# Cross-attention matmul and low-rank feed-forward layer: variance sums of a column in parts, and conversions, additions and low parts divided anew among the engines

## Chip, cores and metric

One core of one Trainium2 chip. The metric is the device time of the kernel in microseconds (us), the median of three runs.

## The reference

Two layers with a layernorm ahead of each (B = 2, 1024 positions, width 2048; everything is float32). The first multiplies the quantized layernorm with a quantized context, the second is a dense product with a bias and a low-rank part of 8 experts of rank 16, of which the two with the highest router probability count for each position:

```python
def fake_quant(x, s, z):                      # 0..255
    return (clip(round(x / s + z), 0, 255) - z) * s

x = x + matmul(fake_quant(_layernorm(x), s1, z1), fake_quant(ctx_4096, s2, z2))

y = _layernorm(x)
probs = softmax(y @ W_router.T)               # 8 experts
w = the two highest probs, divided by their sum
h = einsum('td,erd->ter', y, lora_A)          # r = 16
x = x + y @ W_base.T + b_base + einsum('ter,eor,te->to', h, lora_B, w) * 2.0
```

## The kernel before, in words

**Order of work.** Five programs are written out by hand, one for each engine (`sync_program`, `tensor_program`, `scalar_program`, `vector_program`, `pool_program`): each is a list of calls of small functions, and each function begins with its waits. Tables at the head of the file say which engine does a call that several could do ('a' ScalarE, 'd' VectorE, 'p' GpSimd): `QUANT` and `BACK` (first layer's activations), `CTXQ` and `CONV` (quantization and conversion of the context), `SQ0` and `SUM0` (additions for the second layernorm's statistics), `YLO` and `WLO` (low parts). An engine runs its list strictly in order, so a wait holds up all that stands behind it. SyncE (SP) issues nearly all loads and stores; GpSimd issues the stores of the output and some accumulating transfers on a queue of its own.

**Layer 1.** Batch 0 has 8 tiles of 128 positions, batch 1 too. For each: load (`xn_load`, 512 KB twice), statistics on VectorE (`ln1_stats` L572, L577), coefficients on GpSimd (`ln1_coef` L582 to L592), quantization to uint8 (`ln1_quant`, L606 on ScalarE, L608 on VectorE), 16 transposes of a block of 128 on TensorE (`ln1_turn` L624, four instructions since the uint8 are turned as f32), write-back of the turned tile as bf16 (`ln1_back`, L634 ScalarE, L636 VectorE). The context comes in 32 tiles of 1 MB (`ctx_load`; 16 for a batch), each quantized (`ctx_quant`, L652 ScalarE, L654 VectorE) and converted to bf16 (`ctx_conv`, L661 ScalarE, L663 VectorE and GpSimd). There are two load buffers, two uint8 buffers and two bf16 buffers (and a third for tile 2). `gemm1` (L683) takes 32 products of 512 columns for a tile (two banks of 512 positions, 16 blocks of the width); the first three tiles are done in quarters of 256 positions, as the turned tiles become ready. `evac1` (L698 VectorE, L695 ScalarE) adds the residual to a bank.

**Second layernorm, batch 0.** Beside the later products of layer 1, the 16 tiles of x are summed (`add0`, L713 VectorE, L709 GpSimd) and so are the squares of the values less a shift (`shift0`, `square0` L771, `sqadd0` L779). `mean` (L746) multiplies the sum with a constant matrix; `centre0` (L785) subtracts it from the tiles. `var_total(0)` (L822) multiplies the two sums, block by block, with one column of that matrix: 16 products of one column (32 instructions, f32 takes two each). `var_offset`, `var_add`, `var_root`, `var_diag` and `var_spread` make the scale of each position from them. The norms of the low-rank and router matrices (`a_root`, `r_root`) lie nearby. For batch 1, `var_total(1)` has one sum: 8 products, 16 instructions.

**Layer 2.** Each batch has 8 pairs of 128 + 128 outputs (numbers 0 to 7 and 8 to 15), and each pair is done as a block product of seven instead of eight: the operands of the activations (B11, T1, B21, B22, T2, T3, T4, each 2 MB with both parts) and of the weights are sums and differences (`y_diff` L989 to L1006, `w_add` L1383 to L1396), each split in an fp16 high part (`y_high`, `w_high` L1403, ScalarE) and low part (`y_low` L1013, `w_low` L1409, on VectorE or GpSimd). `product` is 8 blocks by three products of 512 columns (L1451 to L1453), 24 for each of the seven. Weights come by `raw_load` (1 MB), `w_squares` and `w_norm` (L1319) make a norm that `w_total` (L864, TensorE) sums, `w_scale` (L1358) scales. The low-rank product `lora_h` (L1068 to L1070) of the second batch reads 2 MB loads of the operands (`y_load`) that `yd_store` has put away earlier; `tail` adds the low-rank part to a pair, `post` (L1507, L1513, L1515) combines and evacuates, and `store` (L536, GpSimd) sends 512 KB to the output.

## Time and profile before

| | |
|---|---|
| median of three runs | 965.16 us |
| lowest, highest | 964.08, 966.11 us |
| the profiled execution's own time | 965.27 us |
| its span (first to last instruction) | 963.5 us |
| TensorE busy | 926.9 us (96% of the span) |
| VectorE, ScalarE, GpSimd busy | 583.1 (61%), 506.8 (53%), 309.5 us (32%) |
| mean granted TensorE clock | 0.998 of full speed |
| read from HBM, written | 137.44 MB, 56.62 MB |

The profile is of one execution on one core. Times within it are counted from the span's start. Its parts name an instruction by engine, line of the kernel, operation and the tiles that it writes and reads; PE is TensorE, PEld its weight loads, DVE VectorE, ACT ScalarE, POOL GpSimd, SP SyncE. "[2.45 <-DVE S L663]" behind an instruction says that the engine was idle for 2.45 us before it and what ended that: VectorE's line 663 writing tile S. A DMA's time to landing runs from its issue to its last packet.

### The profile page before, as it was taken

The numbers are of one execution on the slowest core, as the hardware profiler recorded it, in microseconds if no ns is written. First come the engines' busy times: TensorE is split into PE (matmuls) and PEld (weight loads), VectorE is DVE, ScalarE is ACT, GpSimd is POOL, SyncE is SP. The second block draws the span as 40 slices with busy tenths as digits, with TensorE's granted clock in tenths as the row PEclk, the third lists the DMA queues.
The fourth block names the chain that finished last, engine by engine and source line by source line (L and its number), as shares of the span: only waits on it lengthen the run. The fifth ranks groups of instructions, "written<-read, shape, count | busy, mean of one in ns | idle before, by whom it ended". The sixth has DMA issues, their size and how long they took to land.

```text
span 963.5 us, 12922 instructions
## 1 busy us (share of the span) xinstructions
PE 926.9 (96%) x4518; PEld 438.4 (45%) x4538; DVE 583.1 (61%) x730; ACT 506.8 (53%) x494; POOL 309.5 (32%) x249
## 2 busy tenths in 40 slices
...
GB/s 309 361 357 363 336 328 326 299 276 292 282 127 106 231 231 229 245 112 260 176 232 265 177 230 186 332 318 237 103 34 116 50 93 65 99 126 71 88 66 44
DMA packets 61444, 197.07 MB, mean 205 GB/s; under 512 B 5696, under 2 KB 22208, under 8 KB 52928
## 3 DMA queue, kind: packets, MB, share of 16 engines
...
HBM read 137.44 MB, written 56.62 MB: 201 GB/s over the span
## 4 chain that ended last, share of the span: by engine, by line
PE 58%; issue 6%; DVE 3%; DMA 2%; POOL 2%; ACT 1%; DVEq 0%; POOLq 0%; ACTq 0%; SPq 0%
PE PS L1451 17%; PE PS L1452 17%; PE PS L1453 17%; PE PS L1464 1%; PE PS L1466 1%; PE PS L1465 1%; DMA out_dram<-Q 1%; PE PS L1144 1%; DMA S<-in_wT_dram 1%; PE PS L1068 1%; PE PS L1069 1%; PE PS L1070 1%; POOL S L1409 1%; DVE S L790 0%; DVE XA L1013 0%
## 5 line engine op out<-in xcount | busy, mean ns | idle before, releaser
L1451 PE MATMUL PS<-XA,Q 128*128 128x512 f16 x384 | 145.6, 379 | 0.0
L1453 PE MATMUL PS<-XA,Q 128*128 128x512 f16 x384 | 145.6, 379 | 0.0
L1452 PE MATMUL PS<-XA,Q 128*128 128x512 f16 x384 | 145.6, 379 | 0.0
L1409 POOL TENSOR_TENSOR S<-S 128x1024 f16<-128x1024 f32 x29 | 64.5, 2228 | 166.8 <-ACT S L1403 166.8
L683 PE MATMUL PS<-Q,S 128*128 128x512 bf16 x502 | 112.5, 382 | 2.9 <-DVE S L698 2.2
L683 PE MATMUL PS<-EX,S 128*128 128x512 bf16 (+1 forms) x534 | 107.1, 359 | 4.0 <-DVE S L663 2.5
L1403 ACT ACTIVATE Q<-S 128x1024 f16<-128x1024 f32 x64 | 66.6, 1050 | 71.4 <-PE PS L1453 29.2
L1358 ACT ACTIVATE S<-S,WC 128x1024 f32<-128x1024 f32 x64 | 70.8, 1138 | 51.2 <-DMA S<-in_wT_dram 35.3
L1451 PE MATMUL PS<-EX,S 128*128 128x512 f16 x256 | 97.0, 379 | 0.1
L1453 PE MATMUL PS<-EX,S 128*128 128x512 f16 x256 | 97.0, 379 | 0.0
L1452 PE MATMUL PS<-EX,S 128*128 128x512 f16 x256 | 97.0, 379 | 0.0
L1409 DVE TENSOR_TENSOR Q<-S,Q 128x1024 f16<-128x1024 f32 x52 | 65.1, 1262 | 41.4 <-ACT Q L1403 41.2
L1403 ACT ACTIVATE S<-S 128x1024 f16<-128x1024 f32 x48 | 49.6, 1050 | 74.7 <-DVE S L1387 26.3
L1507 DVE SCALAR_TENSOR_TENSOR Q<-PS,WC,Q 128x512 f32<-128x512 f32 x36 | 26.9, 749 | 94.4 <-PE PS L1466 77.7
L683 PEld LDWEIGHTS PS<-Q,S 128*128 128x128 bf16 x512 | 50.4, 99 | 64.7 <-issue 4.8
L683 PEld LDWEIGHTS PS<-EX,S 128*128 128x128 bf16 x544 | 53.9, 99 | 54.2 <-DVE S L663 2.8
L652 ACT ACTIVATE S<-S,cst 128x2048 uint8<-128x2048 f32 x31 | 64.4, 2086 | 19.0 <-DMA S<-in_cT_dram 18.7
L536 POOL DMA_DIRECT2D out_dram<-Q x30 | 26.5, 941 | 121.6 <-DVE Q L1515 64.8
L1409 POOL TENSOR_TENSOR Q<-S,Q 128x1024 f16<-128x1024 f32 x12 | 29.5, 2463 | 90.2 <-ACT Q L1403 90.2
L1451 PEld LDWEIGHTS PS<-XA,Q 128*128 128x128 f16 x384 | 37.6, 98 | 45.7 <-issue 1.1
L1453 PEld LDWEIGHTS PS<-XA,Q 128*128 128x128 f16 x384 | 37.6, 98 | 45.3
L1452 PEld LDWEIGHTS PS<-XA,Q 128*128 128x128 f16 x384 | 37.6, 98 | 44.9 <-issue 0.3
...
## 6 DMA issues: line engine op xcount, KB each, us to landing
...
out_dram<-Q POOLq DMA_DIRECT2D x30, 512.0 KB, 5.6
EX<-in_xn_dram SPq DMA_DIRECT2D x24, 512.0 KB, 6.4
...
XA<-in_xT_dram SPq DMA_DIRECT2D x16, 512.0 KB, 8.3
out_dram<-XA SPq DMA_DIRECT2D x16, 512.0 KB, 7.4
out_dram<-S SPq DMA_DIRECT2D x16, 512.0 KB, 4.3
```

The lines of the kernel that those rows point to most:

```text
L536: e.dma_start(outT[b, o], ob[(2 * i + h) % 3], accum_op=ALU.add).then_inc(stored.of(2 * i + h), 16)
L652: e.activation(u8b[g % 2], ctx_f[g % 2], ACT.Identity, bias=z2, scale=inv2).then_inc(ctxq.of(g), 1)
L683: last = e.matmul(bank(a)[:, t0 % 512:t0 % 512 + t1 - t0], q2[q][:, 128 * k:128 * (k + 1)], q1T[b][:, k, t0:t1], start=(k == 0), stop=(k = ...
L1068: e.matmul(bank(banks[n]), hi[:, c], yh(op, k), start=(k == 0 and op != B22), stop=False)
L1069: e.matmul(bank(banks[n]), hi[:, c], yl(op, k), start=False, stop=False)
L1358: e.activation(v, v, ACT.Copy, bias=0.0, scale=w_cols(i)[:, 4:5]).then_inc(w_scaled.of(i, q), 1)
L1403: e.activation(ring[slot_of(i, n)][:, 0:1024], W_SRC[n], ACT.Copy, bias=0.0, scale=1.0).then_inc(w_hi.of(i, n), 1)
L1409: e.tensor_tensor(v[:, 1024:2048], W_SRC[n], v[:, 0:1024], ALU.subtract).then_inc(w_lo.of(i, n), 1)
L1451: e.matmul(bank(bk), wh, yh(op, k), start=(fresh and k == 0), stop=False, skip_group_check=not fresh)
L1452: e.matmul(bank(bk), wh, yl(op, k), start=False, stop=False, skip_group_check=not fresh)
L1453: last = e.matmul(bank(bk), wl, yh(op, k), start=False, stop=(read and k == 7), skip_group_check=not fresh)
L1507: e.scalar_tensor_tensor(dst, src, kk, dst, op0=ALU.mult, op1=ALU.add).then_inc(post_ok.of(i, n), 1)
```

## The change

- `var_total` is split: for batch 0 the sums of the offset become `offset_total(p)`, those of the squares `var_total(0, p)`, for batch 1 `var_total(1, p)`, with p = 0 and 1, each for four blocks. In `tensor_program` the four calls of batch 0 stand in a row, 16 products earlier than before, and the two of batch 1 in a row. What waited for the one signal waits for the ones that it needs.
- SyncE issues the loads of context tiles 0 and 1 directly behind activation tiles 0 to 3, ahead of tile 4; later loads, stores and reloads stand in another order in places.
- ScalarE, VectorE and GpSimd share quantizations, write-backs, conversions, additions, squares' additions and low parts in another way. Calls before and after: VectorE's conversions 7 and 1, context quantizations 1 and 7, write-backs 9 and 5, quantizations 2 and 6, `add0` 0 and 3, `sqadd0` 0 and 4, `w_low` 71 and 97, `y_low` 55 and 42. ScalarE's conversions 18 and 17, context quantizations 31 and 25, write-backs 9 and 13, quantizations 14 and 10. GpSimd's conversions 7 and 14, `add0` 14 and 11, `sqadd0` 15 and 11, `w_low` 41 and 15, `y_low` 9 and 22.
- `warm` is defined and called nowhere. The tables of layer 2 and the programs' other lines are in another order in places; the diff is cut to its core.

```diff
--- before.py
+++ after.py
-QUANT = {'a': [(0, 1), (0, 2), (0, 3), (0, 4), (0, 5), (0, 6), (1, 0), (1, 1), (1, 2), (1, 3), (1, 4), (1, 5), (1, 6), (1, 7)],
-    'd': [(0, 0), (0, 7)]}
-BACK = {'a': [(0, 0, 0), (0, 1, 0), (0, 3, 1), (0, 2, 0), (0, 4, 0), (0, 6, 0), (0, 7, 1), (1, 0, 0), (1, 4, 0)],
-    'd': [(0, 3, 0), (0, 5, 0), (0, 7, 0), (1, 2, 0), (1, 1, 0), (1, 3, 0), (1, 5, 0), (1, 6, 0), (1, 7, 0)]}
-CTXQ = {'a': [0, 2, 3, 4, 5, 6, 7, 8, 9, 10, 11, 12, 13, 14, 15, 16, 17, 19, 18, 20, 21, 22, 23, 24, 25, 26, 28, 27, 29, 30,
-    31], 'd': [1]}
-CONV = {'a': [7, 9, 12, 13, 14, 15, 16, 17, 18, 21, 22, 25, 26, 27, 28, 29, 30, 31], 'd': [0, 2, 3, 6, 10, 11, 23], 'p': [1, 4,
-    5, 8, 19, 20, 24]}
+QUANT = {'a': [(0, 1), (0, 3), (0, 4), (0, 5), (0, 7), (1, 2), (1, 4), (1, 5), (1, 6), (1, 7)], 'd': [(0, 0), (0, 2), (0, 6),
+    (1, 0), (1, 1), (1, 3)]}
+BACK = {'a': [(0, 0, 0), (0, 2, 0), (0, 3, 1), (0, 3, 0), (0, 4, 0), (0, 5, 0), (0, 6, 0), (0, 7, 1), (1, 1, 0), (1, 4, 0),
+    (1, 6, 0), (1, 5, 0), (1, 7, 0)], 'd': [(0, 1, 0), (0, 7, 0), (1, 0, 0), (1, 2, 0), (1, 3, 0)]}
+CTXQ = {'a': [0, 3, 4, 5, 7, 9, 8, 10, 12, 13, 15, 14, 16, 18, 20, 19, 22, 24, 25, 26, 27, 28, 29, 30, 31], 'd': [1, 2, 6, 11,
+    17, 21, 23]}
+CONV = {'a': [3, 7, 8, 9, 11, 14, 15, 17, 19, 20, 22, 23, 25, 26, 28, 29, 30], 'd': [31], 'p': [0, 1, 2, 4, 5, 6, 10, 12, 13,
+    16, 18, 21, 24, 27]}
...
-SQ0 = {'d': [], 'p': [1, 2, 3, 4, 5, 6, 7, 8, 9, 10, 11, 12, 13, 14, 15]}
-SUM0 = {'d': [], 'p': [1, 2, 3, 4, 5, 6, 7, 9, 10, 11, 12, 13, 14, 15]}
+SQ0 = {'d': [1, 3, 7, 11], 'p': [2, 4, 5, 6, 8, 9, 10, 12, 13, 14, 15]}
+SUM0 = {'d': [7, 9, 14], 'p': [1, 2, 3, 4, 5, 6, 10, 11, 12, 13, 15]}
...
     centred1 = signal("centred1", range(NT))
     cd_out = loaded("cd_out", range(NT), 2)
     sq1_ok = signal("sq1", range(1, NT))
-    var_sum = signal("var_sum", range(NB))
+    off_sum = signal("off_sum", range(2))
+    var_sum = signal("var_sum", [(b, p) for b in range(NB) for p in range(2)])
     var_off = signal("var_off", range(2))
     var_eps = signal("var_eps", range(NB))
@@ -640,6 +641,15 @@
             e.wait_ge(*back[b, i, part])
 
 
+    def warm(e, n, at=None):
+        e.wait_ge(*const["mean"])
+        if at is not None:
+            e.wait_ge(*xn_in[0, at, 1])
+        v = mean_w[:, :].bitcast(BF16)[:, 0:128]
+        for _ in range(n):
+            e.matmul(bank(3)[:, 0:128], v, v, start=True, stop=True)
+
+
     def q2_place(g):
         return 2 if g == 2 else g % 2
 
@@ -656,7 +666,8 @@
     def ctx_conv(e, g):
         e.wait_ge(*ctxq[g])
         if g >= 3:
-            e.wait_ge(*gemm[{3: 1, 4: 0}.get(g, g - 2), 1])
+            for h in range(2):
+                e.wait_ge(*gemm[{3: 1, 4: 0}.get(g, g - 2), h])
         if g in CONV["a"]:
             e.activation(q2[q2_place(g)], u8b[g % 2], ACT.Copy, bias=-128.0, scale=1.0).then_inc(conv.of(g), 1)
         else:
@@ -807,7 +818,15 @@
         e.wait_ge(*sq1_ok[i])
         e.tensor_tensor(acc1, acc1, sq1[i % 2], ALU.add).then_inc(acc1_ok.of("sq", i), 1)
 
-    def var_total(e, b):
+    def offset_total(e, p):
+
+        e.wait_ge(*sum0[NT - 1])
+        e.wait_ge(*back[1, 6, 0])
+        for t in range(4 * p, 4 * p + 4):
+            last = e.matmul(bank(4)[:, TT + t:TT + t + 1], acc0[:, 128 * t:128 * (t + 1)], mean_w[:, 0:1], start=True, stop=True)
+        last.then_inc(off_sum.of(p), 1)
+
+    def var_total(e, b, p):
 
         at, acc = (bank(6), acc1) if b else (bank(4), accD)
         if b:
@@ -815,22 +834,21 @@
             e.wait_ge(*centred1[15])
         else:
             e.wait_ge(*sqsum0[15])
-            e.wait_ge(*sum0[NT - 1])
             e.wait_ge(*back[1, 6, 0])
-        for src, c in ((acc, 0),) if b else ((acc, 0), (acc0, TT)):
-            for t in range(TT):
-                last = e.matmul(at[:, c + t:c + t + 1], src[:, 128 * t:128 * (t + 1)], mean_w[:, 0:1], start=True, stop=True)
-        last.then_inc(var_sum.of(b), 1)
+        for t in range(4 * p, 4 * p + 4):
+            last = e.matmul(at[:, t:t + 1], acc[:, 128 * t:128 * (t + 1)], mean_w[:, 0:1], start=True, stop=True)
+        last.then_inc(var_sum.of(b, p), 1)
 
     def var_offset(e):
-        e.wait_ge(*var_sum[0])
+        e.wait_ge(*off_sum[1])
+        e.wait_ge(*var_sum[0, 1])
         e.tensor_scalar(rr[:, TT:2 * TT], bank(4)[:, TT:2 * TT], 1.0, None, op0=ALU.mult).then_inc(var_off.of(0), 1)
         e.wait_ge(*var_off[0])
         e.tensor_tensor(rr[:, TT:2 * TT], rr[:, TT:2 * TT], rr[:, TT:2 * TT], ALU.mult).then_inc(var_off.of(1), 1)
 
     def var_add(e, b):
         if b:
-            e.wait_ge(*var_sum[1])
+            e.wait_ge(*var_sum[1, 1])
             e.tensor_scalar(rr[:, 0:TT], bank(6)[:, 0:TT], EPS, None, op0=ALU.add).then_inc(var_eps.of(1), 1)
         else:
             e.wait_ge(*var_off[1])
@@ -985,7 +1003,7 @@
                 e.wait_ge(*y_lo[0, k - 1, "T"])
                 e.wait_ge(*y_hi[0, k - 1, "T"])
             else:
-                e.wait_ge(*var_sum[0])
+                e.wait_ge(*var_sum[0, 1])
         e.tensor_tensor(TX[:, 512:1024], B[:, 512:1024], A[:, 512:1024], ALU.subtract).then_inc(y_diff.of(b, k, 3), 1)
 
     def y_diff1(e, b, k):
@@ -1045,7 +1063,8 @@
             e.wait_ge(*prod[7, 1])
         else:
             e.wait_ge(*turned[1, 7])
-            e.wait_ge(*var_sum[0])
+            e.wait_ge(*off_sum[1])
+            e.wait_ge(*var_sum[0, 1])
         e.scalar_tensor_tensor(lo[:, v], src[:, v], s_a, hi[:, v], op0=ALU.mult, op1=ALU.subtract).then_inc(a_lo.of(b, c), 1)
 
     def lora_h(e, b, ks):
@@ -1091,7 +1110,7 @@
                                    op0=ALU.mult, op1=ALU.add).then_inc(h_ok.of(b, s), 1)
 
     def r_clear(e):
-        e.wait_ge(*var_sum[0])
+        e.wait_ge(*off_sum[1])
         for s in range(2):
             e.memset(r_ab[0][s], 0.0).then_inc(r_zero.of(s), 1)
 
@@ -1302,7 +1321,7 @@
                 e.wait_ge(*conv[30])
                 e.wait_ge(*conv[31])
                 e.wait_ge(*turned[1, 7])
-                e.wait_ge(*var_sum[0])
+                e.wait_ge(*off_sum[1])
             e.activation(junk, raw[h], ACT.Square, accum_out=col_[:, h:h + 1]).then_inc(w_sq.of(j, h), 1)
         e.wait_ge(*b_in[j])
         if j >= 2:
...
     def sync_program(e, general):
-        xn_load(e, 0, 4); ctx_load(e, 0); ctx_load(e, 1); xn_load(e, 0, 5); ctx_load(e, 2); xn_load(e, 0, 6)
-        xn_load(e, 0, 7); x_load(e, 1, general); ctx_load(e, 3); x_load(e, 0, general); x_load(e, 2, general)
...
+        ctx_load(e, 0); ctx_load(e, 1); xn_load(e, 0, 4); x_load(e, 0, general); xn_load(e, 0, 5); ctx_load(e, 2)
+        xn_load(e, 0, 6); xn_load(e, 0, 7); ctx_load(e, 3); xn_load(e, 1, 0); x_load(e, 2, general); xn_load(e, 1, 1)
+        ctx_load(e, 4); x_load(e, 1, general); x_load(e, 3, general); x_load(e, 4, general); ctx_load(e, 5)
+        xn_load(e, 1, 2); ctx_load(e, 6); xn_load(e, 1, 3); ctx_load(e, 7); x_load(e, 8, general); x_load(e, 7, general)
...
-        yd_store(e, 7, 6); yd_store(e, 7, 1); yd_store(e, 7, 7); yd_store(e, 7, 5); a_reload(e); b_load(e, 8); y_load(e, 0)
+        yd_store(e, 7, 1); a_reload(e); yd_store(e, 7, 2); b_load(e, 8); yd_store(e, 7, 6); yd_store(e, 7, 3)
+        yd_store(e, 7, 5); yd_store(e, 7, 4); yd_store(e, 7, 7); raw_load(e, 8, 1); y_load(e, 0); raw_load(e, 8, 0)
...
     def tensor_program(e):
         ln1_turn(e, 0, 0); ln1_turn(e, 0, 1); ln1_turn(e, 0, 2); ln1_turn(e, 0, 3); gemm1(e, 0, 0, 256, 0, 16)
...
-        gemm1(e, 18, 0, 512, 0, 8); gemm1(e, 18, 512, 1024, 0, 8); var_total(e, 0); gemm1(e, 18, 0, 512, 8, 16)
...
-        tail(e, 2, 1); tail(e, 2, 3); var_total(e, 1); product(e, 3, 0); var_spread(e, 1); product(e, 3, 1)
...
+        gemm1(e, 17, 512, 1024, 8, 16); r_total(e); gemm1(e, 17, 0, 512, 8, 16); offset_total(e, 0); offset_total(e, 1)
+        var_total(e, 0, 0); var_total(e, 0, 1); gemm1(e, 18, 512, 1024, 0, 8); gemm1(e, 18, 512, 1024, 8, 16)
...
+        product(e, 2, 6); tail(e, 2, 1); var_total(e, 1, 0); var_total(e, 1, 1); product(e, 3, 0); var_spread(e, 1)
...
     def scalar_program(e):
-        ln1_quant(e, 0, 1); ln1_back(e, 0, 0, 0); ln1_quant(e, 0, 2); ln1_back(e, 0, 1, 0); ln1_quant(e, 0, 3)
-        ctx_quant(e, 0); ln1_back(e, 0, 3, 1); ln1_back(e, 0, 2, 0); ln1_quant(e, 0, 4); ctx_quant(e, 2); ln1_quant(e, 0, 5)
...
+        ln1_quant(e, 0, 1); ln1_back(e, 0, 0, 0); ctx_quant(e, 0); ln1_quant(e, 0, 3); ln1_back(e, 0, 2, 0)
+        ln1_back(e, 0, 3, 1); ln1_back(e, 0, 3, 0); ln1_quant(e, 0, 4); ln1_quant(e, 0, 5); ln1_back(e, 0, 4, 0)
...
     def vector_program(e):
         ln1_stats(e, 0, 0); ln1_stats(e, 0, 1); ln1_quant(e, 0, 0); ln1_stats(e, 0, 2); ln1_stats(e, 0, 3)
-        ln1_stats(e, 0, 4); ln1_back(e, 0, 3, 0); ctx_conv(e, 0); ctx_quant(e, 1); ln1_stats(e, 0, 5); ln1_stats(e, 0, 6)
-        ctx_conv(e, 2); ln1_stats(e, 0, 7); ln1_back(e, 0, 5, 0); ln1_quant(e, 0, 7); ln1_back(e, 0, 7, 0); evac1(e, 1, 0)
...
+        ln1_quant(e, 0, 2); ln1_back(e, 0, 1, 0); ctx_quant(e, 1); ln1_stats(e, 0, 4); ln1_stats(e, 0, 5); ctx_quant(e, 2)
+        ln1_stats(e, 0, 6); ln1_stats(e, 0, 7); evac1(e, 0, 0); ln1_quant(e, 0, 6); ln1_stats(e, 1, 0); evac1(e, 2, 0)
...
     def pool_program(e, general):
-        ln1_coef(e, 0, 0); ln1_coef(e, 0, 1); ln1_coef(e, 0, 2); ln1_coef(e, 0, 3); ln1_coef(e, 0, 4); ctx_conv(e, 1)
-        ln1_coef(e, 0, 5); ln1_coef(e, 0, 6); ln1_coef(e, 0, 7); ln1_coef(e, 1, 0); ctx_conv(e, 4); ln1_coef(e, 1, 1)
...
+        ln1_coef(e, 0, 0); ln1_coef(e, 0, 1); ln1_coef(e, 0, 2); ln1_coef(e, 0, 3); ctx_conv(e, 0); ctx_conv(e, 1)
+        ln1_coef(e, 0, 4); ln1_coef(e, 0, 5); ctx_conv(e, 2); ln1_coef(e, 0, 6); ln1_coef(e, 0, 7); ln1_coef(e, 1, 0)
...
+        ctx_conv(e, 12); sqadd0(e, 8); ctx_conv(e, 13); add0(e, 10); ln1_coef(e, 1, 7); sqadd0(e, 9); sqadd0(e, 10)
+        add0(e, 11); add0(e, 12); ctx_conv(e, 16); sqadd0(e, 12); add0(e, 13); sqadd0(e, 13); add0(e, 15); ctx_conv(e, 18)
+        sqadd0(e, 14); a_root(e); sqadd0(e, 15); r_clear(e); r_root(e); var_root(e, 0); add1(e, 2); ctx_conv(e, 21)
...
+        w_low(e, 7, 3); store(e, 6, 0); y_low(e, 1, 7, "A"); store(e, 7, 0); store(e, 7, 1); w_low(e, 8, 4); store(e, 8, 1)
...
```

## Rows read from the trace of the kernel before

**Rows 1.** Page, part 1: busy us of each engine (share of the span), instructions:
```profile
PE 926.9 (96%) x4518; PEld 438.4 (45%) x4538; DVE 583.1 (61%) x730; ACT 506.8 (53%) x494; POOL 309.5 (32%) x249
```

**Rows 2.** Waits of TensorE: line waiting <- releaser: us in all, how many, longest:
```profile
PE PS L683 <- DVE S L698: 2.2, 2, 1.2
PE PS L864 <- DVE WC L1319: 2.1, 1, 2.1
```

**Rows 3.** Windows: us; busy PE, PEld, DVE, ACT, POOL; PE clock, DMA share, GB/s:
```profile
0.00:28.91 28.91, 4.47 (x17) 2.87 (x17) 17.98 (x37) 14.49 (x9) 9.08 (x34) 1.00 0.82 297
28.91:60.00 31.09, 30.04 (x234) 24.09 (x236) 25.46 (x37) 20.02 (x11) 12.16 (x27) 1.00 0.97 377
60.00:169.40 109.40, 108.85 (x505) 51.33 (x513) 80.03 (x100) 84.02 (x56) 84.97 (x65) 1.00 0.90 341
622.00:963.50 341.50, 338.19 (x1634) 154.04 (x1632) 127.72 (x146) 109.08 (x119) 60.77 (x38) 1.00 0.40 112
```

**Rows 4.** TensorE's timeline: start, us, instructions in a row [idle before <- releaser]:
```profile
25.34 1.12 PE L624 MATMUL PS<-ident,S 128*128 128x128 f32 x4 [2.63 <-ACT S L606]
...
28.91 9.09 PE L683 MATMUL PS<-EX,S 128*128 128x256 bf16 x64 [2.45 <-DVE S L663]
...
43.80 1.91 PE L683 MATMUL PS<-EX,S 128*128 128x256 bf16 x16 [0.99 <-ACT EX L634]
...
58.16 0.60 PE L624 MATMUL PS<-ident,S 128*128 128x128 f32 x4
...
215.40 20.88 PE L683 MATMUL PS<-Q,S 128*128 128x512 bf16 x94 [0.92 <-DVE S L698]
```

**Rows 5.** Timelines of ScalarE and of VectorE, first 28 us:
```profile
15.70 2.09 ACT L606 ACTIVATE XA<-EX,mv 128x2048 uint8<-128x2048 f32 x1 [9.85 <-POOL mv L592]
17.70 1.85 ACT L634 ACTIVATE EX<-PS 128x2048 bf16<-128x2048 uint8 x1
...
27.17 2.77 ACT L634 ACTIVATE EX<-PS 128x1024 bf16<-128x1024 uint8 x2
...
12.85 1.28 DVE L608 TENSOR_SCALAR S<-EX,mv 128x2048 uint8<-128x2048 f32 x1
...
16.72 2.40 DVE L572 BATCH_NORM_STATS2 st<-XA 128x6 f32<-128x512 f32 x4
```

**Rows 6.** DMA issues, 3 to 6 us: KB each, us to landing:
```profile
XA<-in_xn_dram SPq DMA_DIRECT2D x4, 512.0 KB, 10.1
```

**Rows 7.** Timelines and windows around the variance sums, and GpSimd's last additions:
```profile
157.00 1.96 PE L746 MATMUL PS<-S,mean_w 128*128 128x512 f32 x4
...
169.46 3.73 PE L822 MATMUL PS<-mean_w,S 128*128 128x1 f32 x32
...
169.40:176.30 6.90, 6.66 (x41) 4.80 (x41) 6.83 (x9) 3.52 (x2) 0.00 (x0) 0.75 0.97 354
...
426.00:428.00 2.00, 2.00 (x11) 0.88 (x9) 0.50 (x1) 0.00 (x0) 2.00 (x1) 1.00 0.00 0
...
157.28 4.86 POOL L779 TENSOR_TENSOR S<-S 128x1024 f32<-128x1024 f32 x2 [0.99 <-ACT S L771]
```

**Rows 8.** ScalarE's timeline, the eviction ahead of the norm's squares:
```profile
366.32 0.78 ACT L1513 ACTIVATE Q<-PS,bo,WC 128x512 f32<-128x512 f32 x1 [3.13 <-DMA out_dram<-Q]
```

**Rows 9.** GpSimd's timeline, three stores; DMA issues, 640 to 672 us:
```profile
647.85 2.66 POOL L536 DMA_DIRECT2D out_dram<-Q  x3
...
EX<-yops_dram SPq DMA_DIRECT2D x1, 2048.0 KB, 18.8
```

**Rows 10.** Groups by line and form: busy, mean ns | idle before; and VectorE's timeline:
```profile
L709 POOL TENSOR_TENSOR S<-S,XA 128x1024 f32<-128x1024 f32 x6 | 15.0, 2498 | 7.3 <-DVE XA L698 7.1
...
L663 POOL TENSOR_SCALAR S<-S 128x2048 bf16<-128x2048 uint8 x7 | 13.3, 1898 | 11.0 <-DVE S L654 6.3 <-PE PS L683 4.2 <-ACT S L652 0.4
...
L1387 DVE TENSOR_TENSOR S<-S 128x1024 f32<-128x1024 f32 x1 | 1.2, 1225 | 0.0
...
626.46 3.14 DVE L1387 TENSOR_TENSOR S<-S 128x1024 f32<-128x1024 f32 x1 [12.07 <-POOL Q L1409]
```

642 lines of the change are left out of this document (318 added, 324 removed), and 88 rows, old and new, of tables (EVAC, GEMM, POST, PROD).

## Prediction

> **What bounds the kernel now.** I read the busy line of the page first. TensorE is busy for 926.9 of 963.5 us [rows 1], so another engine changes the time only by making TensorE wait or by ending later than it. What can change is the idle 36.6 us, and the clock that TensorE runs at. Next come its waits: the longest outside the start are 2.2 us in two waits for evictions by VectorE and 2.1 us in one wait for a norm [rows 2]. The windows say where the rest lies [rows 3]: 4.47 us of work in the first 28.91 us, 1.05 us idle up to 60 us, 0.55 us idle in the 109.4 us after that. So 25.5 of the 36.6 us lie before 60 us, and there I expect the change to count. About 3.3 us are the last eviction and store, whose chain stays. The timeline of TensorE gives the shape of the start [rows 4]: the last of four groups of transposes at 25.34, a wait of 2.45 us for VectorE's conversion, 64 quarter-width products from 28.91, an idle 0.99 us before 43.80, then no gap to 58.16.
>
> **The change, part by part.** TensorE gets no new work: two calls of the variance sums become six of half or a quarter of the length, with the same 48 instructions. All else is another order and another sharing out. Durations are from the profiled execution, 965.27 us by its own clock, 0.11 above the median of the three runs; I sum against it and take the 0.11 off.
>
> *The start.* Before, ScalarE alternates quantizations of 2.09 us and write-backs of 1.85 us for the first tiles [rows 5], and the context tile is converted after them. Now VectorE quantizes tile 2 and writes back tile 1, and GpSimd converts context tiles 0 and 1. I replay it with the old durations. VectorE begins the statistics of tile 3 at 16.72 and is through at 19.4 (2.40 and a short aggregation); it quantizes tile 2 in 1.28 us (20.7); it then has 4.1 us to write back tile 1, for which ScalarE took 1.85. ScalarE ends its first quantization at 17.8 and the write-back of tile 0 at 19.6 as before, then takes context tile 0 (21.6) and tile 3 (23.7). GpSimd converts the context tile by 23.5 (1.90 us [rows 10]). The transposes of tile 3, 1.12 us, end at 24.8, and the first products start there instead of at 28.91. The second quarter needs tiles 2 and 3 written back, 1.85 and 2.77 us on ScalarE from 23.7, so 28.3. The 64 products took 9.09 us; with a wait of 0 to 1.2 us in them they end at 33.9 to 35.1, before at 38.0. Behind them two groups of transposes and 32 products (9.09 / 2 = 4.5 us at this rate) cover two write-backs (3.7), so the idle 0.99 goes too. At equal work that is 3.6 to 4.8 us early. I take 3.6, the low end, since the low clock of the first products may stretch over the wait.
>
> This rests on the loads. Before, the first two context loads were issued behind tile 4's, which waits for the first quantization; now they follow tile 3's directly. Loads of tiles 2 and 3 took 10.1 us to land [rows 6], because they stood behind those of tiles 0 and 1: the queue was full. Tile 3's landed by 16.72, when its statistics begin without a wait [rows 5], so it was issued at about 6, and the new ones will be too. If the new ones stay behind them, at 377 GB/s [rows 3] one megabyte takes 2.8 us: tile 3 at about 16, context tile 0 at 19, before ScalarE asks for it at 19.6, tile 4 at 24, when VectorE is free for its statistics. The queue has more to do early and later loads gain as TensorE does.
>
> *From 60 to 169 us* TensorE had 0.55 us idle. Here VectorE gives up six conversions and four write-backs and takes four quantizations, six of the context and seven additions; GpSimd takes seven conversions and gives up the seven additions. A context buffer is free when the tile two before is done, and its conversion is due one tile of products later: 94 products took 20.88 us [rows 4], so 32 take 7.0 us. A conversion of 1.90 and two additions of 2.5 [rows 10] just fit. I cost it at nothing; what it costs uncovered is the second rival.
>
> *The variance sums of batch 0.* 32 instructions of one column took 3.73 us, and the granted clock over the 6.9 us from their start was 0.75 [rows 7], so 1.7 us went at the level of 1.2 GHz instead of 2.4. The new functions split the sums in four parts, but the new order puts the four calls next to each other, with no product between; the same in batch 1, where 16 instructions stood together and the clock stayed at 1.00 behind them [rows 7]. So the lost time stays: 0, between -1.9 (no fall, no idle 0.2 us behind it) and 0. The sums also come 16 products earlier. Their squares were complete at 162.14, 7.3 us ahead. Now GpSimd's last addition stands behind a root that waits for VectorE after the mean: 1.96 us of mean, 1.22 of centring, some 0.7 of column work, 2.43 of addition [rows 7, 10], 6.3 us in all, while TensorE has 24 products (5.3) and the offset half of the sums (1.9), 7.2. It fits by 0.9; uncovered by one more addition it costs 1.6.
>
> *The other waits.* Evictions: VectorE gives up three low parts of the activations in that stage and gets three of the weights: 0, between -2.2 and +2.2. The norm wait of 2.1 us came from an eviction on ScalarE that waited for an output buffer until 366.32 [rows 8], ahead of the squares. The new order keeps that, puts both evictions of the pair in front (+0.7) and calls for the norm three products earlier (+0.7), but GpSimd reaches the store slightly sooner: 0, between -2.1 and +1.4.
>
> *The second low-rank product* is fed by 2 MB loads just ahead of TensorE. Three stores that GpSimd issued at 647.85, behind these loads, made the one beside them take 18.8 us [rows 9], against 8.4 for its own and the megabyte before it at 377 GB/s: 3.5 us for each store. Two of them now go out during the loads that TensorE is waiting for. On the other side the reload ahead of these loads is issued earlier. I take +0.5, between 0 and +3.5.
>
> *Low parts.* 26 of the weights' 41 on GpSimd go to VectorE and 13 of the activations' the other way. VectorE is busy for 127.72 of the last 341.5 us [rows 3]; nothing.
>
> **Sum:** -3.6 + 0.5 = -3.1; 965.27 - 3.1 - 0.11 = 962.1 us.
>
> **Where rule and trace part.** GpSimd's additions took 2.5 us on average, and one of VectorE 3.14 where the same line took 1.22 elsewhere, while GpSimd worked beside it [rows 10]: a collision costs up to 1.9 us, and few show. The Trainium skill, "SBUF — State Buffer", section "Who interferes with whom", says that a VectorE instruction with two SBUF inputs and a GpSimd instruction that reads SBUF shut each other out for a whole instruction, which speaks against sharing work out between these two. By that rule any overlap in the first 170 us counts, and the term set at nothing above would be some us, as in the second rival.
>
> **Rivals.** (1) *The gain is given back at a later wait*, the low-rank product's or an eviction's. For: loads with no slack. Against: the earlier reload. 962.1 + 2.3 = 964.4. (2) *Conversions on GpSimd become TensorE's wait; slower.* Place: context tiles 4 to 21. Behind two additions (5.0), the factors of a tile (1.7) and one collision (1.9), a conversion of 1.9 ends 10.5 us after its release, 3.5 late. Two such cases give 962.1 + 7.0 = 969.1. Point: a single one leaves 965.6, no change. Against: the new order rarely puts two additions there. (3) *The early context loads share the queue with tiles 2 and 3* instead of standing behind them: 2 MB, up to 5.6 us later for tile 3, and the start gains nothing or loses 1: 962.1 + 4 = 966.1. Against: loads queued behind others did land in turn. (4) *The clock does not fall after the sums* though they stand together, as in batch 1: 962.1 - 1.9 = 960.2. That the announced split does not take place is part of the forecast.
>
> **Chances.** Forecast 0.44 (its own range 959.9 to 963.6), rival 1 0.20, 2 0.14, 3 0.08, 4 0.14. A measurement of this kernel tells 0.2%, 1.9 us, from no change. Faster: nearly all of the forecast and the fourth, 0.56; slower: the second and half of the third, 0.18; same: the rest, 0.26. The range leaves out the far end of the second rival and gains beyond both bounds: 957.8 to 968.0.
>
> **What would show it.** Right: first product at 24.5 to 26 us, no idle before 44, all 32 sums in a row at about 163 us and 1.2 GHz behind them. Wrong: product waits released by GpSimd's conversions; waits of the second low-rank product for loads; statistics of tile 2 or 3 that wait for their load.

## The result, and the profile after it

The changed kernel takes 973.04 us (median of 13 runs, 967.86 to 977.63), the kernel before 966.11 us (13 runs): a ratio of 1.0068, with a 95% interval of 1.0045 to 1.0090. It is slower by 0.7%, where I forecast faster by 0.3%.

The busy line of the changed kernel's page, against [rows 1]:

```profile
PE 930.1 (96%) x4538; PEld 438.5 (45%) x4538; DVE 622.7 (64%) x750; ACT 491.7 (51%) x487; POOL 277.3 (29%) x236
```

Its waits of TensorE (line that waits, what released it: us in all, times, longest), against [rows 2]:

```profile
PE PS L1087 <- DMA XA<-yops_dram: 5.3, 2, 4.9
PE PS L694 <- DVE S L709: 4.6, 1, 4.6
...
PE PS L882 <- DVE WC L1338: 1.5, 1, 1.5
PE PS L1087 <- ACT S L706: 1.4, 1, 1.4
PE PS L1087 <- DVE S L709: 1.2, 1, 1.2
```

The profiled execution's span is 971.4 us, 7.9 more than before. Idle time outside TensorE's work is 971.4 - 930.1 = 41.3 us, 4.7 more than before, although the start is shorter. The other 3.2 us are in the busy time itself: the same work at a lower clock. The windows show both (columns as in [rows 3]: stretch, its us, busy PE, PEld, DVE, ACT, POOL, clock, DMA share, GB/s):

```profile
0.00:25.09 25.09, 4.26 (x17) 3.00 (x18) 18.70 (x33) 10.18 (x6) 10.61 (x30) 1.00 0.92 349
...
60.00:162.00 102.00, 101.67 (x478) 47.65 (x476) 78.92 (x92) 73.91 (x51) 74.59 (x59) 1.00 0.90 342
...
225.00:276.00 51.00, 43.73 (x191) 18.88 (x189) 43.40 (x48) 33.15 (x33) 24.46 (x13) 0.93 0.79 258
...
622.00:971.40 349.40, 340.70 (x1636) 154.33 (x1634) 148.94 (x166) 110.25 (x120) 16.12 (x17) 1.00 0.38 109
...
230.00:240.00 10.00, 5.39 (x16) 2.00 (x16) 9.11 (x11) 4.63 (x7) 3.71 (x3) 0.66 1.03 360
638.59:642.60 4.01, 4.01 (x11) 1.50 (x12) 0.80 (x1) 0.00 (x0) 0.00 (x0) 0.57 1.05 399
```

The first 170 us are as good as forecast. The time goes in two places, near 230 us and near 638 us, and each has a stretch of low clock behind it. TensorE's timeline says where it stands at each point:

```profile
24.18 1.11 PE L625 MATMUL PS<-ident,S 128*128 128x128 f32 x4 [2.55 <-ACT S L607]
25.09 8.48 PE L694 MATMUL PS<-EX,S 128*128 128x256 bf16 x64
...
35.27 0.66 PE L625 MATMUL PS<-ident,XA 128*128 128x128 f32 x4 [1.26 <-ACT XA L607]
...
162.17 1.84 PE L826 MATMUL PS<-mean_w,S 128*128 128x1 f32 x16
163.88 1.93 PE L839 MATMUL PS<-mean_w,S 128*128 128x1 f32 x16
165.66 20.88 PE L694 MATMUL PS<-Q,S 128*128 128x512 bf16 x96
186.62 1.95 PE L739 MATMUL PS<-S,mean_w 128*128 128x512 f32 x4
188.41 41.60 PE L694 MATMUL PS<-Q,S 128*128 128x512 bf16 x192
234.62 37.05 PE L694 MATMUL PS<-Q,S 128*128 128x512 bf16 x160 [4.61 <-DVE S L709]
272.89 0.38 PE L1087 MATMUL PS<-XA,S 128*128 128x512 f16 x1 [1.22 <-DVE S L709]
...
275.14 0.39 PE L1087 MATMUL PS<-XA,S 128*128 128x512 f16 x1 [1.44 <-ACT S L706]
...
638.59 0.42 PE L1087 MATMUL PS<-XA,Q 128*128 128x512 f16 x1 [4.92 <-DMA XA<-yops_dram]
```

First products: 25.09 for 28.91 us, 3.8 ahead. In this execution no half clock follows the sums. At 230.0 us the wait begins. The 160 products behind it took 37.05 us; 96 of them took 20.88 from 165.66, which is 34.8 for 160. (The 94 in 20.88 us of [rows 4] are 96 too, with two records missing.) The clock events of the trace (its two levels are 1.2 and 2.4 GHz) show 1.2 GHz for 6.8 us from 233 us and for 3.4 us from 639 us, and nowhere else between 28 us, where the first event raises the clock, and the end. Half of 10.2 us is 5.1 us, of which some fell into the waits themselves.

At 230 us VectorE had this behind it (its timeline):

```profile
222.63 2.95 DVE L1031 TENSOR_TENSOR XA<-S,XA 128x1024 f16<-128x1024 f32 x1
225.50 4.36 DVE L1128 SCALAR_TENSOR_TENSOR S<-Braw,cst,S 128x128 f16<-128x128 f32 x1
229.78 1.21 DVE L983 TENSOR_TENSOR S<-XA,PS 128x1024 f32<-128x1024 f32 x1
...
233.07 1.40 DVE L709 SCALAR_TENSOR_TENSOR S<-PS,cst,S 128x512 f32<-128x512 f32 x2
```

GpSimd's timeline beside it:

```profile
211.34 1.09 POOL L518 DMA_DIRECT2D S<-in_xT_dram  x1 [0.37 <-issue]
...
222.14 2.35 POOL L733 TENSOR_TENSOR S<-S 128x1024 f32<-128x1024 f32 x1 [7.52 <-DMA S<-in_xT_dram]
...
225.41 2.43 POOL L1031 TENSOR_TENSOR EX<-S,EX 128x1024 f16<-128x1024 f32 x1
227.54 2.16 POOL L674 TENSOR_SCALAR S<-S 128x2048 bf16<-128x2048 uint8 x1
```

`r_low` (L1128), a tile of 128 by 128, starts when GpSimd starts a low part and ends when the conversion behind it ends: 4.36 us. Ahead of it another VectorE operation stretched to 2.95 us over GpSimd's addition. The two evictions of context tile 25, for which TensorE waits, stand behind.

### The profile page after: what moved, and what is told of

It reads as the page before. It is cut to its first block, busy times and chain, and to the rows that moved or that the text cites. A ratio compares the mean times of both kernels' runs of the same rounds, so it can differ in the third digit from the quotient of the medians.

```text
span 971.4 us, 12949 instructions
## 1 busy us (share of the span) xinstructions
PE 930.1 (96%) x4538; PEld 438.5 (45%) x4538; DVE 622.7 (64%) x750; ACT 491.7 (51%) x487; POOL 277.3 (29%) x236
## 4 chain that ended last, share of the span: by engine, by line
PE 42%; DMA 3%; issue 3%; DVE 1%; POOL 1%; ACT 0%; SPq 0%; DVEq 0%; POOLq 0%
PE PS L1470 12%; PE PS L1471 12%; PE PS L1472 12%; DMA XA<-yops_dram 2%; PE PS L1483 1%; PE PS L1485 1%; PE PS L1484 1%; DMA S<-in_wT_dram 1%; PE PS L1163 0%; POOL S L1031 0%; PE PS L1088 0%; PE PS L1087 0%; PE PS L1089 0%; DVE Q L1068 0%; DVE S L1007 0%
## 5 line engine op out<-in xcount | busy, mean ns | idle before, releaser
L1428 DVE TENSOR_TENSOR Q<-S,Q 128x1024 f16<-128x1024 f32 x55 | 71.3, 1304 | 63.0 <-ACT Q L1422 63.0
L1428 DVE TENSOR_TENSOR S<-S 128x1024 f16<-128x1024 f32 x42 | 50.4, 1220 | 17.1 <-ACT S L1422 17.0
L662 ACT ACTIVATE S<-S,cst 128x2048 uint8<-128x2048 f32 x25 | 52.1, 2086 | 15.0 <-DMA S<-in_cT_dram 12.8
L1534 DVE TENSOR_SCALAR Q<-PS,WC,bo 128x512 f32<-128x512 f32 x27 | 21.8, 807 | 42.7 <-PE PS L1485 21.5
```

The costliest lines, as they stand in the source:

```text
L662: e.activation(u8b[g % 2], ctx_f[g % 2], ACT.Identity, bias=z2, scale=inv2).then_inc(ctxq.of(g), 1)
L1428: e.tensor_tensor(v[:, 1024:2048], W_SRC[n], v[:, 0:1024], ALU.subtract).then_inc(w_lo.of(i, n), 1)
L1534: e.tensor_scalar(dst, src, kk, bcol, op0=ALU.mult, op1=ALU.add).then_inc(post_ok.of(i, n), 1)
```

## The experiments

Sixteen kernels, in the order in which they ran; lines of an edit are cut to the calls that move. "Clock" is the mean over a kernel's runs of the granted clock. Where it is set against a time, the loss is (1 - clock) times the span: for the changed kernel's 13 runs 6.4 us at a mean clock of 0.9935; for the kernel before, in the 26 runs shared by the first four experiments, 2.7 us at 0.9972. So of the 7 us between them up to 3.7 are clock: where a fall lies over a wait it costs nothing.

Each ratio is against runs of the kernel before taken beside that kernel; their medians were 966.7 (e1 to e4), 965.1 (e5 to e8), 966.4 (e9 to e11), 965.3 (e12 to e14) and 964.7 us (e15, e16), so medians of different groups can be up to 2 us apart for no reason of the kernels, and the ratios are the safer comparison. The profiled execution is one run of its kernel and not always a typical one: those of e4_start (959.0 us), e5 (973.2) and e10 (963.7) are the fastest of their kernels, that of e11 (973.8) the slowest, and that of e16 (972.4) is 6.8 us above its median. One of e7's 12 runs took 3760.9 us; it is left out of its clock, and leaving it out of the median changes 0.01 us.

| kernel | median us | ratio to before (95%) | clock |
|---|---|---|---|
| changed | 973.0 | 1.0068 (1.0045 to 1.0090) | 0.9935 |
| e1_evac | 975.5 | 1.0076 (1.0049 to 1.0103) | 0.9920 |
| e2_stores | 970.6 | 1.0041 (1.0015 to 1.0067) | 0.9937 |
| e3_both | 971.5 | 1.0051 (1.0025 to 1.0076) | 0.9945 |
| e4_start | 962.7 | 0.9957 (0.9932 to 0.9981) | 0.9978 |
| e5_rlow | 978.6 | 1.0141 (1.0115 to 1.0168) | 0.9912 |
| e6_rlow_st | 972.3 | 1.0074 (1.0045 to 1.0103) | 0.9935 |
| e7_split | 971.2 | 1.0061 (1.0041 to 1.0082) | 0.9960 |
| e8_oldearly | 967.4 | 1.0012 (0.9991 to 1.0034) | 0.9970 |
| e9_sp | 976.6 | 1.0100 (1.0073 to 1.0128) | 0.9907 |
| e10_sp_st | 971.1 | 1.0040 (1.0019 to 1.0061) | 0.9946 |
| e11_sp_st_split | 967.9 | 1.0015 (0.9994 to 1.0035) | 0.9969 |
| e12_start_split | 958.9 | 0.9930 (0.9909 to 0.9951) | 0.9993 |
| e13_split_before | 962.3 | 0.9970 (0.9950 to 0.9989) | 0.9998 |
| e14_split_after | 972.6 | 1.0066 (1.0040 to 1.0092) | 0.9942 |
| e15_layer2 | 969.9 | 1.0051 (1.0029 to 1.0073) | 0.9949 |
| e16_layer1 | 965.6 | 1.0005 (0.9977 to 1.0034) | 0.9948 |

**The start alone (e4_start).** The kernel before with the new start; of its edits, the lines of SyncE and of VectorE:

```diff
-        xn_load(e, 0, 4); ctx_load(e, 0); ctx_load(e, 1); xn_load(e, 0, 5)
+        ctx_load(e, 0); ctx_load(e, 1); xn_load(e, 0, 4); xn_load(e, 0, 5)
-        ln1_stats(e, 0, 4); ln1_back(e, 0, 3, 0); ctx_conv(e, 0); ctx_quant(e, 1)
+        ln1_quant(e, 0, 2); ln1_back(e, 0, 1, 0); ctx_quant(e, 1); ln1_stats(e, 0, 4)
```

> The kernel before with the start of the changed one alone: context loads 0 and 1 issued ahead of activation tile 4, VectorE quantizes tile 2 and writes back tile 1, ScalarE writes back tile 3 whole, GpSimd converts context tiles 0 and 1; all later sharing as before. Theory: first product at about 25.1 us instead of 28.9, context stage 3 to 4 us earlier, and the time 966.1 - 3.7 = 962.5 us unless the loads near 630 us take it back. Rival (the rest of the new sharing is needed to keep it): the gain at 60 us is there but gone by 170 us, time within 1 us of 966.

962.69 us, as expected, and a ratio clear of 1. The first products in TensorE's timeline of e4_start:

```profile
25.23 8.44 PE L683 MATMUL PS<-EX,S 128*128 128x256 bf16 x64
```

Its waits for evictions:

```profile
PE PS L683 <- DVE S L698: 1.8, 2, 1.2
```

The gain of the start is kept to the end: with the old order behind it there is no late eviction and no late load.

**Evictions and r_low (e1_evac, e3_both, e5_rlow, e6_rlow_st).** On VectorE of the changed kernel, e1:

```diff
-        y_low(e, 0, 2, "A"); r_low(e); y_scale(e, 0, 3, "A")
-        y_diff3(e, 0, 3); y_diff1(e, 0, 3); y_diff2(e, 0, 3); evac1(e, 25, 1); evac1(e, 25, 0)
+        y_low(e, 0, 2, "A"); evac1(e, 25, 1); evac1(e, 25, 0); r_low(e); y_scale(e, 0, 3, "A")
+        y_diff3(e, 0, 3); y_diff1(e, 0, 3); y_diff2(e, 0, 3)
```

> The changed kernel with both evictions of context tile 25 moved ahead of r_low and of the four y_ calls behind it on VectorE; nothing else. Theory (the eviction stood in the wrong place behind a VectorE instruction held up by GpSimd, and the idle time then cost clock): the 4.61 us wait at 230 us is gone or below 1 us, no stretch of half clock at 233 us, and at most the 5.3 us wait for loads near 638 us is longer than before; 973.0 - 4.6 - 2.6 = 966 us, or 1 to 3 us more where the loads take it back. Rival (VectorE is simply behind with its work in this stretch): the wait only moves to a later eviction or to the low-rank product at 272 us, and the time stays within 2 us of 973.

The rival held: the wait moved on, and the time is 975.5 us, 0.8 above the changed kernel by the ratios (2.5 by the medians, where it allowed 2). VectorE's timeline in e1:

```profile
232.58 1.41 DVE L709 SCALAR_TENSOR_TENSOR S<-PS,cst,S 128x512 f32<-128x512 f32 x2 [5.01 <-PE PS L694]
233.91 0.34 DVE L1128 SCALAR_TENSOR_TENSOR S<-Braw,cst,S 128x128 f16<-128x128 f32 x1
```

TensorE's:

```profile
244.23 29.49 PE L694 MATMUL PS<-Q,S 128*128 128x512 bf16 x128 [3.03 <-ACT S L672]
```

I had put the evictions too early: VectorE idled for 5.01 us on products that were not there yet, and TensorE's wait went to 1.62 us here, 3.03 for a conversion and 2.31 for an eviction later. One thing it shows by the way: without GpSimd beside it, `r_low` takes 0.34 us. e3 is e1 with the edit of e2:

> Both edits in the changed kernel: evictions of tile 25 early and the two stores late. Theory: both gains add up, 973.0 - 7.2 - 6.2 = about 960 us, 962 if half of one is taken back by the loads; faster than the kernel before (966) by 0.3 to 0.6%, because the gain at the start and at the variance sums is then kept. Rival (gains of an early stage are always taken back at the second low-rank product): no better than the better of the two single edits, 966.

The theory fell here too: 971.5, no better than e2_stores. e5 puts `r_low` behind the evictions instead, and e6 adds the stores' edit:

```diff
-        y_low(e, 0, 2, "A"); r_low(e); y_scale(e, 0, 3, "A")
+        y_low(e, 0, 2, "A"); y_scale(e, 0, 3, "A")
...
-        y_diff2(e, 0, 3); evac1(e, 25, 1); evac1(e, 25, 0); add1(e, 9)
+        y_diff2(e, 0, 3); evac1(e, 25, 1); evac1(e, 25, 0); r_low(e); add1(e, 9)
```

> The changed kernel with r_low moved from ahead of y_scale(0, 3, A) to behind the two evictions of context tile 25, on VectorE; nothing else. Theory (r_low, 0.34 us by itself in the first two experiments, took 4.36 us in the changed kernel because GpSimd ran a low part of 2.43 us and a conversion of 2.16 us beside it; the eviction behind it was late by that much): r_low takes under 1 us unless it meets another GpSimd operation, the evictions of tile 25 start about 4 us earlier, the wait of 4.61 us at 230 us is below 1 us and the half clock behind it is gone; mean granted clock of the runs 0.995 to 0.997 instead of 0.9935; 973.0 - 4.4 - 2.4 = 966 to 967 us. Rival (the backlog of VectorE or of the residual transfers in this stage sets the time, as when the evictions were moved too early): another wait of 3 us takes its place and the time stays above 971.

> As e5_rlow, and the two stores held back behind the fifth load as in e2_stores. Theory: the two gains add, e2_stores' 970.6 less 4 to 7 = 964 to 966 us, at or below the kernel before (966.7). Rival as for e5_rlow: stays at 970.

`r_low` took 0.34 us in both, and both stayed slow (978.6 and 972.3 us), as the rival says. e5 is even slower than the changed kernel, with a ratio of 1.0141 for 1.0068 and intervals that do not meet; its profiled execution, the fastest of its five runs, does not show why. In it another VectorE operation, 0.69 us elsewhere, is stretched beside GpSimd's conversion; then VectorE waits 1.06 us for the residual load of tile 25 and starts the evictions at 232.96, as late as before the edit:

```profile
229.11 2.07 DVE L1012 TENSOR_TENSOR S<-S 128x512 f32<-128x512 f32 x1
...
232.96 1.41 DVE L709 SCALAR_TENSOR_TENSOR S<-PS,cst,S 128x512 f32<-128x512 f32 x2 [1.06 <-DMA S<-in_xT_dram]
```

So the collision was real but covered: the residual load, queued on SyncE behind other work, was as late as VectorE.

**The transfers of tiles 23 to 25 (e9_sp, e10_sp_st, e11_sp_st_split).** GpSimd's accumulating load of residual tile 23, issued at 211.34 us, took 10.7 us to land (its addition waited to 222.14, above); in e4_start, issued at 211.50, 5.8 us. SyncE's `keep(23)` and all behind it waited for it.

```diff
-        x_load(e, 24, general); ctx_load(e, 27); keep(e, 23); ctx_load(e, 28); x_load(e, 25, general)
+        x_load(e, 24, general); keep(e, 23); ctx_load(e, 27); x_load(e, 25, general); ctx_load(e, 28)
```

> The changed kernel with SyncE's order ctx_load(27), keep(23), ctx_load(28), x_load(25) made keep(23), ctx_load(27), x_load(25), ctx_load(28); nothing else. Theory (the first cause of the wait at 230 us lies in the transfers: context load 27 and residual load 24 were issued at 211.1 to 211.7 us, with GpSimd's accumulating load of residual tile 23 at 211.3, which so landed after 10.7 us instead of 5.8 as in e4_start; GpSimd's addition and low part behind it, 4.9 us late, then fell beside r_low, and keep(23), x_load(25) stood behind it on SyncE): the accumulating load takes 5 to 7 us, r_low under 1 us at the place it has, x_load(25) is issued 4 us earlier, the wait of 4.61 us is below 1.5 us; time 973.0 - 3.5 - 2 = 967 to 968 us. Rival (the order of these transfers only shifts the wait to tile 26 to 28, as in the other experiments): waits of 4 us and more in all between 225 and 276 us, time above 971.

> As e9_sp, with the two stores held back as in e2_stores. Theory: e2_stores' 970.6 less 5 = 964 to 966 us. Rival: 970.

Right on the steps, wrong on the time: the load took 6.9 us, `r_low` 0.34 at its old place, the eviction wait was 1.14 us. But later waits of the stage (1.29, 0.33, 0.76, 1.31 us) took its place, 4.8 us in all, and the times are no better than without the edit: 976.6 and 971.1 us. That is the rival.

**The stores among the loads (e2_stores, e8_oldearly).** In the changed kernel, GpSimd:

```diff
-        store(e, 7, 0); store(e, 7, 1); w_low(e, 8, 4); store(e, 8, 1)
+        w_low(e, 8, 4); e.wait_ge(*y_in[4]); store(e, 7, 0); store(e, 7, 1); store(e, 8, 1)
```

> The changed kernel with the stores (7, 0) and (7, 1) on GpSimd held back until the fifth load for the second low-rank product has landed (w_low(8, 4) ahead of them). Theory (these two stores, 1 MB, take the place of the third load): third load lands 5.3 to 5.5 us behind the second instead of 10.3, the 4.92 us wait and the half clock behind it (3.4 us, 1.7 lost) are gone; 973.0 - 4.9 - 1.7 + up to 0.5 = 966.5 us. Rival (the loads are late for another reason, the later issue of the first): the wait shrinks by less than 2 us and the time stays above 971.

And the counter-test, one store moved early in the kernel before:

```diff
-        w_low(e, 8, 1); w_low(e, 8, 0); w_low(e, 8, 4)
+        w_low(e, 8, 1); store(e, 6, 1); w_low(e, 8, 0); w_low(e, 8, 4)
...
-        store(e, 7, 1); store(e, 6, 1); store(e, 7, 0)
+        store(e, 7, 1); store(e, 7, 0)
```

> The kernel before with one store, (6, 1), moved from 648 us to behind GpSimd's first low part of pair 8, at about 626.5 us, among the loads for the second low-rank product. Theory (half a megabyte stored there moves the load in flight by 2.4 us): the third or fourth load lands about 2.4 us later than now, TensorE waits 1 to 1.5 us for it at 632 to 640 us where it waited nowhere before; time 966.7 + 1.2, and up to 1.7 more where the clock falls: 968 to 969.5. Rival (the loads have enough slack, the stores cost nothing by themselves): no wait, 966.7.

When the 2 MB loads for the second low-rank product land, from the landing events of each trace (us):

```
               1st     2nd     3rd     4th    stores beside them
before       616.49  625.81  631.24  636.66   none
changed      617.06  628.19  638.45  643.87   two, landing 634.84 and 638.18
e2_stores    619.54  628.76  634.16  639.59   none
e8_oldearly  620.04  629.64  635.05  642.81   one, landing 638.26
```

A load follows the one ahead in 5.4 us; with two stores beside it in 10.3, with one in 7.8: 2.4 us for each half megabyte. In e2 the wait is gone, in e8 there is one of 1.45 us where there was none. (All loads of e8 land later than before, the first by 3.6 us; 2.4 us earlier its fourth would still have come ahead of TensorE.) What it does in the time is less clear. From the changed kernel to e2 it is 2.5 us, less than the 6.5 that were expected, and the two intervals overlap; the same edit gives 4.0, 6.3 and 5.5 us in e1 to e3, e5 to e6 and e9 to e10. The mean clock of e2 (0.9937) is hardly above the changed kernel's (0.9935), although in its profiled execution the half clock near 639 us is gone with the wait. e8 is not told from the kernel before, at 967.4 us where 968 to 969.5 was expected. The wait in TensorE's timeline of e8:

```profile
642.86 0.39 PE L1068 MATMUL PS<-XA,Q 128*128 128x512 f16 x1 [1.45 <-DMA XA<-yops_dram]
```

**The variance sums really split (e7, e11, e12, e13, e14).** e7 is e6, and e11 is e10, with this; e14 is the changed kernel with it alone:

```diff
-        offset_total(e, 0); offset_total(e, 1)
-        var_total(e, 0, 0); var_total(e, 0, 1); gemm1(e, 18, 512, 1024, 0, 8); gemm1(e, 18, 512, 1024, 8, 16)
-        gemm1(e, 18, 0, 512, 0, 8); gemm1(e, 18, 0, 512, 8, 16)
+        offset_total(e, 0); gemm1(e, 18, 512, 1024, 0, 8); offset_total(e, 1); gemm1(e, 18, 512, 1024, 8, 16)
+        var_total(e, 0, 0); gemm1(e, 18, 0, 512, 0, 8); var_total(e, 0, 1); gemm1(e, 18, 0, 512, 8, 16)
```

> As e6_rlow_st, with the four calls of the variance sums of batch 0 really put between products: 8 products of tile 18 after each. If the stretch of half clock behind the sums (3.4 us at 166.7 us, in four of the seven profiled executions so far; 1.7 us lost) comes of 32 one-column instructions in a row, it does not appear and the mean clock of the runs rises by about 0.001; time 0.5 to 1.5 us below e6_rlow_st. Rival (it does not depend on the placing, or the later sums make VectorE wait): time and clock the same within 1 us.

> As e10_sp_st, with 8 products of tile 18 after each of the four variance calls of batch 0. If the one-column sums in a row are what the clock falls behind, the mean clock is 0.001 to 0.002 above e10_sp_st's, no half clock near 167 us, and the time 1 to 1.5 us lower; otherwise both are the same within 1 us.

e13 and e12 do the same in the kernel before and in e4_start: four parts of `var_total(0)`, the first behind the products of tile 17, 8 products between two parts.

> The kernel before with the start of the changed one (as e4_start) and its variance sums of batch 0 really split: four parts of four blocks, 8 products of tile 18 between two parts. Theory (two gains that are independent): e4_start's 962.7 less 0.5 to 1.5 us of clock = 961.2 to 962.2 us, mean clock 0.998 to 0.999; faster than both kernels. Rival (the split costs more in fill and drain of one-column products between full ones than the clock gives back): 963 to 964.

> The kernel before with the variance sums of batch 0 split in four parts between products, nothing else. Theory (the sums in a row bring the fall): no half clock at 170 to 177 us, mean clock 0.998 instead of 0.9973, time 0.5 to 1.5 us below 966.4. Rival (the fall has another cause and comes anyway): clock 0.9973 and time the same within 0.5 us.

> The changed kernel with its four calls of the variance sums put between products (8 products of tile 18 behind each), nothing else. Theory: mean clock rises from 0.9935 to 0.9955 as between e10_sp_st and e11_sp_st_split, time 973.0 - 2 = 971 us; the waits at 230 and 638 us stay. Rival (the falls come of the waits alone): clock and time as before this edit, 973.

The kernel before gains 0.3% by it, and with the new start 0.7%: 958.9 us, the best of all, faster than both kernels. The split gives 3.1 us in e13 and 3.8 from e4_start to e12, where 0.5 to 1.5 was expected; the mean clocks account for 2.4 and 1.5 of them, and the rest is open. Eleven of the 12 runs of e13 show a clock of 1.000, one 0.998; of the 17 runs of the kernel before beside them one does. In the changed family the pair e10 and e11 agrees (0.9946 to 0.9969, 3.2 us), e6 and e7 less (1.1 us), and e14 gains nothing to speak of. The stretch in e12:

```profile
162.27 0.95 PE L823 MATMUL PS<-mean_w,S 128*128 128x1 f32 x8
163.65 1.90 PE L683 MATMUL PS<-Q,S 128*128 128x512 bf16 x8 [0.43 <-ACT S L661]
165.38 0.95 PE L823 MATMUL PS<-mean_w,S 128*128 128x1 f32 x8
...
171.26 13.97 PE L683 MATMUL PS<-Q,S 128*128 128x512 bf16 x64
```

Of the 18 profiled executions there are, 13 have the sums in a row, and 9 of these show 1.2 GHz right behind them or across their end (3.4 or 6.8 us); of the five with split sums none does. Rival: the waits alone. In e14 they remain (3.56 and 4.84 us) with 6.8 us of half clock across the end of each, and none behind the sums; so waits and sums each go with falls of their own.

**Crosswise (e15_layer2, e16_layer1).** The two orders are cut at the first low-rank product on each engine. e15 has the first part of e4_start and the second of the changed kernel, e16 the first part of the changed kernel and the second of the kernel before; calls that one has ahead of the cut and the other behind are done once.

> Layer 1 and the operands of batch 0 in the order and sharing of e4_start (the kernel before with the new start, sums in a row), everything behind the first low-rank product as in the changed kernel. Theory (layer 2 costs the wait for the third load, 4.9 us, and half clock behind it, 1.7 us; nothing else of it costs): e4_start's 962.7 + 6 to 7 = 969 us; no waits over 1.3 us between 60 and 290 us. Rival (the loads wait only because TensorE comes earlier or because of what layer 1 leaves behind): 963 to 965.

> Layer 1 and the operands of batch 0 as in the changed kernel, everything behind the first low-rank product as in the kernel before. Theory (layer 1's order costs the waits between 225 and 276 us, 4 to 7 us, and half clock of 2 to 3 us behind them, against a gain of 3.7 at the start): 973.0 - 6.5 = 966 to 967 us, about the kernel before's; mean clock 0.995 to 0.996. Rival (layer 1's waits are a matter of how far TensorE is ahead and would be as in e4_start): 962 to 963.

Both about as expected: 969.9 and 965.6 us (966 to 967 for the second). The largest wait in TensorE's timeline of e15, for the loads:

```profile
633.57 0.58 PE L1036 MATMUL PS<-XA,Q 128*128 128x512 f16 x1 [3.42 <-DMA XA<-yops_dram]
```

And in that of e16, for evictions of layer 1:

```profile
233.04 2.52 PE L643 MATMUL PS<-Q,S 128*128 128x512 bf16 x8 [1.98 <-DVE S L658]
275.03 0.53 PE L1036 MATMUL PS<-XA,S 128*128 128x512 f16 x1 [4.32 <-DVE S L658]
```

By the medians, the start gives 4.0 us (966.7 to 962.7), the rest of layer 1 costs 2.9 (962.7 to 965.6) and layer 2 costs 7.2 (962.7 to 969.9): 966.7 - 4.0 + 2.9 + 7.2 = 972.8, and the changed kernel has 973.0. By the ratios, each good to about a quarter of a per cent, the two costs are 4.6 and 9.1 us, and the sum comes to 1.0099 where the changed kernel has 1.0068: 3 us too much. That they add up so well by the medians is luck. Layer 2's cost is clear of the noise; for layer 1 the intervals of e4_start and e16 just overlap.

## Why the prediction was wrong

**The start: right.** Forecast 24.8 us for the first product and 3.6 us gained; 25.09 and 3.8 in the profile, 4.0 in the time of e4_start. The loads stayed in turn (rival 3 fell). The idle 0.99 us before 43.80 went, as forecast; the transposes of tile 5 wait 1.26 us instead, behind the first 64 products and just over the 1.2 us allowed within them, so "no idle before 44" did not hold. The working's own numbers add up to 3.9 to 5.1 us (38.0 less 35.1 or 33.9, and the idle 0.99), not to 3.6 to 4.8; the profile's 3.8 lies in the stated range and just under the other.

**From 60 to 162 us: right.** 0.33 us idle. The second rival, conversions on GpSimd, did not happen there: no wait of the changed kernel is released by L674.

**The evictions: the step that failed first.** "Evictions: VectorE gives up three low parts of the activations in that stage and gets three of the weights: 0, between -2.2 and +2.2." Counting what moved said nothing about the order. Between 225 and 276 us TensorE waits 4.61, 1.22 and 1.44 us, where the kernel before has two waits of 1.24 and 0.45: 5.6 us more, with 2.2 as the bound. Shown: the collision with `r_low`, the accumulating load that took 10.7 us for 5.8, the residual load as late as VectorE, and that removing the first or shortening the second moves the wait on. e16, with layer 1's new order and layer 2's old one, has waits of this kind again (in a profiled execution at the slow end of its runs) and is 2.9 us above e4_start. Which of the many changes in layer 1 makes VectorE and the loads late there stays open, as does the order that would clear it; e4_start shows only that the old one does.

**The second low-rank product: right in mechanism, mis-sized.** "I take +0.5, between 0 and +3.5." The store's price was too high (3.5 forecast, 2.4 measured for each half megabyte), the slack of the loads too large: I took one store's price as the bound, while both fell in front of the third load, and the reload issued earlier gave nothing, since the loads behind it were issued later (first load landed at 617.06 for 616.49). 4.92 us of wait. e15 puts layer 2's whole cost at 7 us or more; the wait and half of the 3.4 us at 1.2 GHz behind it make 6.6 in the changed kernel's profile and 5.1 in e15's, and holding the stores back gave 2.5 to 6.3 us. What is left is open.

**The clock: a term that was missing.** I priced every wait at its idle time. All 14 waits of more than 3 us outside the start, in the 18 profiled executions, have 3.4 or 6.8 us at 1.2 GHz behind or across their end, and so have 9 of the 17 waits of 2 to 3 us. So a wait of 4.6 to 4.9 us cost up to 3.4 us more. By the mean clocks this is up to 3.7 of the 7 us. That falls come with waits is what the traces show; no experiment adds or takes away a wait alone, and e2 took one away with no clear change in the mean clock. The profiled execution of the kernel before had waits of at most 2.1 us after the start, and showed nothing of this.

**The variance sums: right that the announced split doesn't take place, and the price was there.** I counted the 1.7 us as a loss that stays, with 1.9 for the opposite case. Where the sums are truly split the kernel before gains 3.1 us (0.3%). The changed kernel's own profiled execution has no fall behind its sums; that was one of 4 in 13, and no effect of its order (rival 4 fell).

**The rule that I set against the trace.** Here the trace agrees with the Trainium skill, "SBUF — State Buffer", section "Who interferes with whom": a VectorE instruction with two inputs in SBUF is locked out while GpSimd reads SBUF. The measured price is 4.36 us for an instruction of 0.34, over two GpSimd operations that came back to back; the most that I had allowed was 1.9. In the time it was covered by a load. The forecast of 0.56 for faster rested on all small terms being zero on average; rival 1 (gain given back at an eviction or a load) is what happened, at both places: from e4_start's 962.7 to 973.0 us it gives back 10.3 us, where I had priced it at 2.3 and given it a chance of 0.20.
